# Computing one layer for half the tokens with the tokens in the partitions

## The chip, the cores and the metric

The kernel runs on one core of a Trainium2 chip. The metric is the time of one execution on the device in microseconds (us); the median of three runs is taken. Engines: TensorE (PE; PEld is its weight load), VectorE (DVE), ScalarE (ACT), GpSimd (POOL) and SyncE (SP), which issues the DMAs here.

## What is computed

x has 1024 tokens of 256 features, in float32. Block 1 is a gated layer in which one matrix per expert, ctx_2048[e] (256 x 256), is gate, up and down weight alike; the expert follows from the token's id. Block 2 is a mixture of 16 experts with 96 hidden features, top 4, and a shared expert.

```python
def _L0_xattn_ref(hidden_states, token_ids, Wg, Wu, Wd):      # all three are ctx_2048
    expert_ids = jnp.minimum(tid // tokens_per_expert, E - 1)  # E = 4
    for e in range(E):
        g = jax.nn.silu(jnp.einsum('bsd,fd->bsf', hidden_states, Wg[e]))
        u = jnp.einsum('bsd,fd->bsf', hidden_states, Wu[e])
        y = jnp.einsum('bsf,df->bsd', g * u, Wd[e])
        out = jnp.where((expert_ids == e)[..., None], y, out)
    return out
x = x + _L0_xattn_ref(_layernorm(x, axis=-1), itok_BxS_13_99985, ctx_2048, ctx_2048, ctx_2048)
x = x + _L0_ffn_ref(_layernorm(x, axis=-1), ...)   # sigmoid router, top 4, 16 experts and a shared one
```

Gate and up have the same weights, so layer 1 of block 1 is one product z = W x, from which silu(z) * z is made; layer 2 multiplies that by W again.

## The kernel before

**Tiling.** Tokens are handled in two halves of 512 (h = 0, 1), feature-major: 128 features (m or k = 0, 1) in the partitions, 512 tokens in the columns. Every product has both operands split into a high part rounded for the fast matmul (hi) and the rest (lo): three matmuls hi x hi, lo x hi, hi x lo for each k. The low parts of the weights are made by GpSimd (low_part(n), one for each piece of weights that was loaded), the high parts by ScalarE (high_part(n)).

**Block 1.** The list mixes gives the order of (layer, half, output features m): (1,0,0), (1,0,1), (1,1,0), (2,0,0), (2,0,1), (1,1,1), (2,1,0), (2,1,1). For a mix n TensorE (mix(n)) makes z for each of the 4 experts in a bank of its own, in a ring of 6 PSUM banks (ring_order); ScalarE copies the first expert's (first_z), VectorE puts the others over it where the id is beyond a threshold (pick: copy_predicated, one instruction of 512 columns for each of 3 experts, in a chain). In layer 1 follow silu (silu_z), the product (hidden_product), and the split into h_hi (hidden_high on ScalarE or hidden_cast on VectorE) and h_lo (hidden_low). In layer 2 the residual is added into xt, x with the features in the partitions (add_block_1).

**The norm ahead of block 2, half 0.** It needs tokens in the partitions: TensorE turns x1 (x1_transposes, 8 transposes, inside mix(5)), VectorE takes statistics (tile_stats, layer_norm_vars), GpSimd makes rstd (rstd_of(2)), VectorE and ScalarE normalise two tiles each (layer_norm_apply, apply_norm), and TensorE turns them back (norm_transposes, behind mix(6)'s k = 0 matmuls). Half 1's goes over HBM (turn_x1, write_x1, read_x1, turn_xn, write_xn, read_xn) while block 2 runs. The tile x[:, TT:] serves as the buffer of both turns.

**Block 2.** 26 items (half, chunk of hidden features), in the order (0,0) to (0,10), (1,0), (0,11), (0,12), (1,1) and so on; for item g TensorE does 12 matmuls of gate and up, then the 6 down matmuls of item g - 2. SyncE's queue runs up to 4 items ahead (spread_rows). output(0) adds half 0's result to xt at item 15.

**What sets the order.** Each engine's instructions stand in a list written out by hand; engines wait on semaphores by count. GpSimd's list in the stretch concerned is: low_part(4) to (6), a wait for x1_done (both tiles of half 0's layer 2), low_part(7), rstd_of(2), a wait for xlo_done, further low parts. A piece's load waits until its slot of 4 is free (w_hi, w_lo).

## Time and profile before

| | us |
|---|---|
| median of 3 runs (169.48 to 169.74) | 169.66 |
| the profiled execution | 169.34 |
| its span, first to last instruction | 167.2 |
| TensorE busy, 705 matmuls | 162.5 |
| VectorE busy, 237 instructions | 114.5 |
| ScalarE busy, 116 instructions | 68.7 |
| GpSimd busy, 36 instructions | 37.2 |

The granted TensorE clock was 1.00 throughout. A timeline row has the start, the duration, the engine, the line of the kernel, the operation with output<-inputs, and how many instructions were merged; behind it in brackets stands how long the engine was idle just before, and for whom. Matmuls overlap each other, so their cost is the distance of their starts. All times within the profiled execution are counted from the span's start.

### The profile page before, as it was taken

The numbers are of one execution on the slowest core, as the hardware profiler recorded it, in microseconds if no ns is written. First come the engines' busy times: TensorE is split into PE (matmuls) and PEld (weight loads), VectorE is DVE, ScalarE is ACT, GpSimd is POOL, SyncE is SP. The second block draws the span as 40 slices with busy tenths as digits, with TensorE's granted clock in tenths as the row PEclk, the third lists the DMA queues.
The fourth block names the chain that finished last, engine by engine and source line by source line (L and its number), as shares of the span: only waits on it lengthen the run. The fifth ranks groups of instructions, "written<-read, shape, count | busy, mean of one in ns | idle before, by whom it ended". The sixth has DMA issues, their size and how long they took to land.

```text
span 167.2 us, 2186 instructions
## 1 busy us (share of the span) xinstructions
PE 162.5 (97%) x705; PEld 128.9 (77%) x705; DVE 114.5 (68%) x237; ACT 68.7 (41%) x116; POOL 37.2 (22%) x36
## 2 busy tenths in 40 slices
PE   7999999999999999999999999999999999999992
PEld 2788888888778888888888878888888888888880
DVE  1889999666957998779986744967714444444462
ACT  3654342831359134536734538452222222222210
POOL 1384000656241045556970000000000000000000
PEclk9999999999999999999999999999999999999999
DMA  5891380164304065987225400025441112200003
GB/s 172 275 408 44 107 291 0 21 206 161 115 4 127 16 205 192 219 240 211 67 61 163 153 0 4 1 103 165 173 141 67 63 63 63 65 0 0 4 0 125
DMA packets 12199, 18.78 MB, mean 112 GB/s; under 512 B 3772, under 2 KB 6044, under 8 KB 12060
## 3 DMA queue, kind: packets, MB, share of 16 engines
q1 hardware_dynamic: 12188, 18.64, 34.9%
q8 instruction: 6, 0.10, 0.2%
q14 instruction: 5, 0.04, 0.1%
HBM read 16.39 MB, written 2.24 MB: 111 GB/s over the span
## 4 chain that ended last, share of the span: by engine, by line
PE 95%; DMA 2%; DVE 1%; DVEq 0%; issue 0%
PE bank L1030 23%; PE bank L1131 15%; PE bank L1129 13%; PE bank L1130 13%; PE bank L1149 7%; PE bank L1152 7%; PE bank L1150 7%; DMA first<-first_d 2%; PE bank L998 1%; PE bank L1071 1%; PE bank L1065 1%; PE bank L1126 1%; PE bank L1125 1%; PE bank L987 1%; PE bank L1078 1%; PE bank L1060 1%
## 5 line engine op out<-in xcount | busy, mean ns | idle before, releaser
L1131 PE MATMUL bank<-xn_lo,gu_hi 128*128 128x512 f32 (+1 forms) x104 | 41.1, 395 | 0.0
L1129 PE MATMUL bank<-xn_hi,gu_lo 128*128 128x512 f32 x96 | 38.0, 396 | 0.0
L1130 PE MATMUL bank<-xn_hi,gu_hi 128*128 128x512 f32 x96 | 38.0, 396 | 0.0
L599 ACT ACTIVATE h_hi<-hid 128x512 fp32r<-128x512 f32 (+1 forms) x26 | 16.4, 632 | 45.6 <-DVE hid L860 45.6
L865 DVE TENSOR_TENSOR h_lo<-hid,h_hi 128x512 fp32r<-128x512 f32 (+1 forms) x26 | 18.0, 691 | 14.9 <-ACT h_hi L599 14.9
L1131 PEld LDWEIGHTS bank<-xn_lo,gu_hi 128*128 128x128 f32 (+1 forms) x104 | 19.4, 187 | 4.9
L589 ACT ACTIVATE act_sb<-bank 128x512 f32<-128x512 f32 (+1 forms) x26 | 15.4, 592 | 17.5 <-PE bank L1131 17.4
L472 POOL TENSOR_TENSOR gu_lo<-stage,gu_hi 128x512 fp32r<-128x512 f32 x12 | 17.2, 1457 | 21.7 <-ACT gu_hi L504 16.3
L1129 PEld LDWEIGHTS bank<-xn_hi,gu_lo 128*128 128x128 f32 x96 | 18.0, 188 | 4.4
L1130 PEld LDWEIGHTS bank<-xn_hi,gu_hi 128*128 128x128 f32 x96 | 18.0, 188 | 4.3
L749 DVE COPY_PREDICATED prod<-beyond,bank 128x512 f32<-128x512 uint8 x24 | 17.6, 737 | 5.1 <-PE bank L1030 4.4
L1149 PE MATMUL bank<-h_hi,wd_lo 128*128 128x512 f32 (+1 forms) x52 | 20.6, 396 | 0.0
L1150 PE MATMUL bank<-h_hi,wd_hi 128*128 128x512 f32 (+1 forms) x52 | 20.6, 395 | 0.0
L1152 PE MATMUL bank<-h_lo,wd_hi 128*128 128x512 f32 (+1 forms) x52 | 20.5, 395 | 0.0
L860 DVE TENSOR_TENSOR hid<-prod,bank 128x512 f32<-128x512 f32 x24 | 16.5, 688 | 2.0
L847 DVE TENSOR_TENSOR prod<-act_sb,ids 128x512 f32<-128x512 f32 x12 | 9.6, 796 | 8.6 <-ACT act_sb L589 8.6
L847 DVE TENSOR_TENSOR prod<-act_sb,first 128x512 f32<-128x512 f32 x12 | 10.0, 832 | 6.3 <-ACT act_sb L589 5.7
L1030 PE MATMUL bank<-h_hi,ctx_hi 128*128 128x512 f32 x32 | 12.7, 398 | 0.0
L1030 PE MATMUL bank<-h_lo,ctx_hi 128*128 128x512 f32 x32 | 12.7, 395 | 0.0
L1030 PE MATMUL bank<-h_hi,ctx_lo 128*128 128x512 f32 x32 | 12.7, 395 | 0.0
L1152 PEld LDWEIGHTS bank<-h_lo,wd_hi 128*128 128x128 f32 (+1 forms) x52 | 9.8, 188 | 2.4
L1150 PEld LDWEIGHTS bank<-h_hi,wd_hi 128*128 128x128 f32 (+1 forms) x52 | 9.8, 188 | 2.3
(102 smaller groups left out, 213.2 us busy)
## 6 DMA issues: line engine op xcount, KB each, us to landing
stage<-gu_d SPq DMA_DIRECT2D x6, 512.0 KB, 3.9
stage<-wd_d SPq DMA_DIRECT2D x3, 512.0 KB, 4.3
first<-comb_d SPq DMA_DIRECT2D x8, 192.0 KB, 2.9
ids<-comb_d SPq DMA_DIRECT2D x8, 192.0 KB, 3.3
stage<-ctx_d SPq DMA_DIRECT2D x4, 256.0 KB, 6.0
xt<-xt_d SPq DMA_DIRECT2D x1, 1024.0 KB, 9.9
first<-comb_d SPq DMA_DIRECT2D x8, 128.0 KB, 3.0
ids<-comb_d SPq DMA_DIRECT2D x8, 128.0 KB, 2.9
```

The source lines that it names most:

```text
L472: ins = nc.gpsimd.tensor_tensor(lo[:, s], st[:, s], hi[:, s].bitcast(F32), ALU.subtract)
L749: nc.vector.copy_predicated(prod[:, n % 2], beyond[:, e - 1, h * HALF:(h + 1) * HALF], ring_bank("z", n, e)[:]).then_inc(z_picked, 1)
L847: nc.vector.tensor_tensor(prod[:, g % 2], act_sb[:, g % 2], rows, ALU.mult).then_inc(prod_done, 1)
L860: nc.vector.tensor_tensor(hid[0:w, g % 2], src, up_bank(g)[0:w, :], ALU.mult).then_inc(hid_done, 1)
L865: nc.vector.tensor_tensor(h_lo[0:w, slot[g]], hid[0:w, g % 2], h_hi[0:w, slot[g]].bitcast(F32), ALU.subtract).then_inc(hlo_done, 1)
L1030: return nc.tensor.matmul(ring_bank("z", n, e)[:], (ctx_hi, ctx_lo)[a][:, m, e, k], parts[k][b], start=start, stop=stop)
L1129: nc.tensor.matmul(out[:], gu_lo[:, cols], xn_hi[:, h, k], start=(k == 0), stop=False)
L1130: nc.tensor.matmul(out[:], gu_hi[:, cols], xn_hi[:, h, k], start=False, stop=False)
L1131: ins = nc.tensor.matmul(out[0:rows, :], gu_hi[:, wide], xn_lo[:, h, k], start=False, stop=(k == KC - 1))
L1149: nc.tensor.matmul(acc[k][:], wd_lo[0:w, c, cols], hi, start=(c == 0), stop=False)
L1150: nc.tensor.matmul(acc[k][:], wd_hi[0:w, c, cols], hi, start=False, stop=False)
L1152: ins = nc.tensor.matmul(acc[k][:], wd_hi[0:w, c, cols], lo, start=False, stop=(c == ITEMS - 1))
```

## The change

Layer 2 of half 0 is computed with the tokens in the partitions (row_mix): a tile of the hidden activations of 128 tokens is the stationary operand and ctx of two experts (512 columns) the moving one, so for each of 4 tiles t there are 2 banks ("rows", t, pair) with 6 matmuls each. Mixes (2,0,0) and (2,0,1) leave the list, which has 6 entries now, so the former mix(5) is mix(3), mix(6) is mix(4) and mix(7) is mix(5). The picks of half 0's layer 2 work on rows: 3 instructions of 256 columns for each of 4 tiles, into x1_rows, with a mask of one column broadcast over the features (beyond_rows, from id_rows, which is loaded). x itself comes in rows too (x_rows_d, loaded into the part of xt that half 0 used), and add_rows adds it.

The 8 transposes of x1 are gone; statistics and normalisation read x1_rows in SBUF where they read PSUM. The tokens are in another order in the row tiles: hidden tiles of half 0 are written in four-way runs of 32 columns (hidden()), and the norm transposes write their PSUM columns in runs of 32.

The last sum of half 0 needs x1 feature-major: turn_x0 (8 transposes of 128 x 128 on VectorE at the ends of items 8 and 9), write_x0 (4 DMAs at item 12 of SyncE's list), read_x0 (4 DMAs at item 13), and output(0) waits for them. GpSimd's wait ahead of low_part(7) is for all 4 tiles of rows (row_added). On VectorE, pick(3) of experts 1 and 2 stands ahead of layer_norm_apply(2) and that of expert 3 behind it; on ScalarE silu_z(3) stands behind apply_norm(2).

```diff
+X0_TURN, X0_WRITE, X0_READ = 8, 12, 13
...
+        x1_rows = sb("x1_rows", [P, TT, D])
+        id_rows = sb("id_rows", [P, TT], I32)
+        beyond_rows = sb("beyond_rows", [P, E1 - 1, TT], U8)
...
+        turn_d = nc.dram_tensor("turn_d", (QUARTERS, KC, LANES, HALF), F32, kind="Internal").ap()
...
-                      ("x1", 0, 0, 4), ("x1", 0, 1, 5), ("n2", 0, 0, 4), ("n2", 0, 1, 5)]
+                      ("n2", 0, 0, 4), ("n2", 0, 1, 5)]
...
-        ring_order = [("z", n, e) for n in range(7) for e in range(E1)]
-        ring_order += [("gate", 0, 0), ("up", 0, 0)] + [("z", 7, e) for e in range(E1)]
...
+        ring_order = [("z", n, e) for n in range(3) for e in range(E1)]
+        ring_order += [("rows", t, pair) for t in range(TT) for pair in range(2)]
+        ring_order += [("z", n, e) for n in (3, 4) for e in range(E1)]
+        ring_order += [("gate", 0, 0), ("up", 0, 0)] + [("z", 5, e) for e in range(E1)]
...
+            elif what == "rows" and e == 0:
+                eng.wait_ge(row_first, n + 1)
+                eng.wait_ge(row_picked, n * (E1 - 1) + 1)
+            elif what == "rows":
+                eng.wait_ge(row_picked, (n + 1) * (E1 - 1))
...
+        def hidden(tile, b, at):
+
+            if b >= KC:
+                return tile[:, at]
+            order = "p (b t j) -> p b t j" if tile is hid else "p (t b j) -> p b t j"
+            return tile[:, at].rearrange(order, t=TT, j=LANES)
...
-        mixes = [(1, 0, 0), (1, 0, 1), (1, 1, 0), (2, 0, 0), (2, 0, 1), (1, 1, 1), (2, 1, 0), (2, 1, 1)]
+        mixes = [(1, 0, 0), (1, 0, 1), (1, 1, 0), (1, 1, 1), (2, 1, 0), (2, 1, 1)]
...
-            if n != HALVES:
-                return x[:, n % HALVES * TT + t]
-            at = t % (TT // KC) * D
-            return side_bank("x1", 0, t // (TT // KC))[:, at:at + D]
+            return x1_rows[:, t] if n == HALVES else x[:, n % HALVES * TT + t]
...
-            sp.dma_start(xt[:], xt_d).then_inc(xt_in, 16)
+            sp.dma_start(xt[:, :, HALF:], xt_d[:, :, HALF:]).then_inc(xt_in, 16)
+            sp.dma_start(id_rows[:], id_rows_d).then_inc(id_rows_in, 16)
+            sp.dma_start(xt[:, :, 0:HALF], x_rows_d).then_inc(x_rows_in, 16)
...
+            def write_x0():
+                sp.wait_ge(x0_turned, TT)
+                rows = turn_d.rearrange("q k i (b c) -> b i (q k) c", c=P)
+                blocks = x[:, TT:].rearrange("p t d -> p (t d)").rearrange("p (m c) -> p m c", c=P)
+                for b in range(QUARTERS):
+                    sp.dma_start(rows[b], blocks[b * LANES:(b + 1) * LANES]).then_inc(x0_out, 16)
+
+            def read_x0():
+                sp.wait_ge(x0_out, QUARTERS * 16)
+                rows = turn_d.rearrange("q k i n -> q i k n")
+                for q in range(QUARTERS):
+                    sp.dma_start(xt[q * LANES:(q + 1) * LANES, :, 0:HALF], rows[q]).then_inc(x0_back, 16)
...
+                if g == X0_WRITE:
+                    write_x0()
+                if g == X0_READ:
+                    read_x0()
...
-            pool.wait_ge(x1_done, KC)
+            pool.wait_ge(row_added, TT)
             low_part(E1 + 3)
             rstd_of(2)
...
+            def row_z(t):
+
+                act.wait_ge(row_done, 2 * t + 1)
+                nc.scalar.activation(x1_rows[:, t], ring_bank("rows", t, 0)[:, 0:D], ACT.Copy).then_inc(row_first, 1)
...
+                if n == HALVES:
+                    act.wait_ge(row_added, TT)
...
-                nc.scalar.activation(h_hi[:, b], hid[:, b % 2], ACT.Copy).then_inc(h1_high, 1)
+                nc.scalar.activation(hidden(h_hi, b, b), hidden(hid, b, b % 2), ACT.Copy).then_inc(h1_high, 1)
...
-            first_z(3)
+            row_z(0)
             silu_z(2)
             hidden_high(2)
+            row_z(1)
             high_part(4)
             high_part(5)
+            row_z(2)
             high_part(6)
-            first_z(4)
+            row_z(3)
             high_part(7)
             high_part(8)
             router_low_rows()
-            first_z(5)
-            silu_z(5)
+            first_z(3)
             apply_norm(2)
+            silu_z(3)
             x_high("n2", 0, 0)
             x_high("n2", 0, 1)
-            first_z(6)
+            first_z(4)
             router_logits(0)
             score(0)
             silu_gate(0)
-            first_z(7)
+            first_z(5)
             hid_high(0)
...
-                    dve.wait_ge(side_done, side_at["x1", 0, t // (TT // KC)] + 1)
+                    dve.wait_ge(row_added, t + 1)
...
+            def row_thresholds():
+
+                dve.wait_ge(id_rows_in, 16)
+                for e in range(1, E1):
+                    nc.vector.tensor_scalar(beyond_rows[:, e - 1], id_rows[:], float(e * PER_EXPERT), None,
+                                            ALU.is_ge).then_inc(rows_masked, 1)
+
+            def pick_rows(t, experts=range(1, E1)):
+
+                dve.wait_ge(row_first, t + 1)
+                dve.wait_ge(rows_masked, E1 - 1)
+                for e in experts:
+                    dve.wait_ge(row_done, 2 * t + e // 2 + 1)
+                    if e > 1:
+                        dve.wait_ge(row_picked, t * (E1 - 1) + e - 1)
+                    z = ring_bank("rows", t, e // 2)[:, e % 2 * D:(e % 2 + 1) * D]
+                    nc.vector.copy_predicated(x1_rows[:, t], beyond_rows[:, e - 1, t:t + 1].to_broadcast([P, D]),
+                                              z).then_inc(row_picked, 1)
+
+            def add_rows(t):
+
+                dve.wait_ge(row_picked, (t + 1) * (E1 - 1))
+                dve.wait_ge(x_rows_in, 16)
+                residual = xt[:, t * D // HALF, t * D % HALF:][:, 0:D]
+                nc.vector.tensor_tensor(x1_rows[:, t], x1_rows[:, t], residual, ALU.add).then_inc(row_added, 1)
+
+            def turn_x0(first):
+
+                dve.wait_ge(xn_out, QUARTERS * 16)
+                blocks = x[:, TT:].rearrange("p t d -> p (t d)").rearrange("p (q k t i) -> p t k q i", k=KC, t=TT, i=LANES)
+                for t in range(first, first + 2):
+                    for k in range(KC):
+                        ins = nc.vector.transpose(blocks[:, t, k],
+                                                  x1_rows[:, t, k * P:(k + 1) * P].rearrange("p (q i) -> p q i", i=LANES))
+                    ins.then_inc(x0_turned, 1)
...
-                nc.vector.tensor_scalar(h_hi[:, b], hid[:, b % 2], 1.0, None, ALU.mult).then_inc(h1_high, 1)
+                nc.vector.tensor_scalar(hidden(h_hi, b, b), hidden(hid, b, b % 2), 1.0, None, ALU.mult).then_inc(h1_high, 1)
...
-                nc.vector.tensor_tensor(h_lo[:, b], hid[:, b % 2], h_hi[:, b].bitcast(F32),
+                nc.vector.tensor_tensor(hidden(h_lo, b, b), hidden(hid, b, b % 2), hidden(h_hi, b, b).bitcast(F32),
...
+                if h == 0:
+                    dve.wait_ge(x0_back, QUARTERS * 16)
...
+            row_thresholds()
             pick(2, masked[1])
-            pick(3, masked[0], [1])
+            pick_rows(0, [1])
             hidden_product(2)
-            pick(3, masked[0], [2])
+            pick_rows(0, [2])
             hidden_low(2)
-            pick(3, masked[0], [3])
-            add_block_1(3)
-            pick(4, masked[0])
+            pick_rows(0, [3])
+            add_rows(0)
+            for t in range(1, TT):
+                tile_stats(2, t - 1)
+                pick_rows(t)
+                add_rows(t)
+            tile_stats(2, TT - 1)
+            layer_norm_vars(2)
+            pick(3, masked[1], [1, 2])
+            layer_norm_apply(2)
+            pick(3, masked[1], [3])
+            hidden_product(3)
+            hidden_cast(3)
+            hidden_low(3)
+            x_low("n2", 0, 0)
+            x_low("n2", 0, 1)
+            pick(4, masked[1], [1])
+            turn_logits(0)
+            pick(4, masked[1], [2])
+            normalise_scores(0, mark_best(0))
+            pick(4, masked[1], [3])
             add_block_1(4)
             pick(5, masked[1], [1])
-            for t in range(TT):
-                tile_stats(2, t)
-            layer_norm_vars(2)
+            hidden_2(0)
             pick(5, masked[1], [2, 3])
-            layer_norm_apply(2)
-            hidden_product(5)
-            hidden_cast(5)
-            hidden_low(5)
-            x_low("n2", 0, 0)
-            x_low("n2", 0, 1)
-            pick(6, masked[1], [1])
-            turn_logits(0)
-            pick(6, masked[1], [2])
-            normalise_scores(0, mark_best(0))
-            pick(6, masked[1], [3])
-            add_block_1(6)
-            pick(7, masked[1], [1])
-            hidden_2(0)
-            pick(7, masked[1], [2, 3])
-            add_block_1(7)
+            add_block_1(5)
             hid_low(0)
             for g in range(1, N):
...
+                if X0_TURN <= g < X0_TURN + TT // 2:
+                    turn_x0((g - X0_TURN) * 2)
...
-                        ins = nc.tensor.transpose(banks[k][:, t * P:(t + 1) * P], xn[:, t, k * P:(k + 1) * P],
-                                                  consts_sb[:, 0:P])
+                        out = banks[k][:, t * P:(t + 1) * P]
+                        if n == HALVES:
+                            out = banks[k][:].rearrange("p (b t j) -> p t b j", t=TT, j=LANES)[:, t]
+                        ins = nc.tensor.transpose(out, xn[:, t, k * P:(k + 1) * P], consts_sb[:, 0:P])
...
-            def x1_transposes(h, pair):
...
+            def row_mix():
+
+                hi, lo = ([w[:, b].rearrange("p (t c) -> p t c", c=P) for b in range(KC)] for w in (h_hi, h_lo))
+
+                def moving(w, pair, k):
+                    return w[:, :, 2 * pair:2 * pair + 2, k].rearrange("p m e f -> p e m f")
+
+                for t in range(TT):
+                    for pair in range(2):
+                        wait_ring_read(pe, "rows", t, pair)
+                        out = ring_bank("rows", t, pair)[:].rearrange("p (e m f) -> p e m f", e=2, m=KC)
+                        for k in range(KC):
+                            if t == 0 and pair == 0:
+                                pe.wait_ge(h1_high, k + 1)
+                            nc.tensor.matmul(out, hi[k][:, t], moving(ctx_hi, pair, k), start=(k == 0), stop=False)
+                            nc.tensor.matmul(out, hi[k][:, t], moving(ctx_lo, pair, k), start=False, stop=False)
+                            if t == 0 and pair == 0:
+                                pe.wait_ge(h1_done, k + 1)
+                            ins = nc.tensor.matmul(out, lo[k][:, t], moving(ctx_hi, pair, k), start=False, stop=(k == KC - 1))
+                        ins.then_inc(row_done, 1)
 
...
-            for n in range(2, 5):
-                mix(n)
-            mix(5, {1: lambda: (x1_transposes(0, 0), x1_transposes(0, 1))})
-            mix(6, features=[0])
+            mix(2)
+            row_mix()
+            mix(3)
+            mix(4, features=[0])
             norm_transposes("n2", 2, 0)
-            mix(6, experts=[0, 1], features=[1])
+            mix(4, experts=[0, 1], features=[1])
             gate_or_up(0, False)
             gate_or_up(0, True)
-            mix(6, experts=[2, 3], features=[1])
-            mix(7)
+            mix(4, experts=[2, 3], features=[1])
+            mix(5)
...
+        "id_rows_d": ids[0:HALF].reshape(QUARTERS, TT, LANES).transpose(0, 2, 1).reshape(P, TT),
+        "x_rows_d": a["x"].reshape(TOKENS, D)[0:HALF].reshape(QUARTERS, TT, LANES, D).transpose(0, 2, 1, 3).reshape(P, KC, HALF),
```

## Rows read from the trace of the kernel before

**Rows 1.** The page, part 1: busy us (share of span) and instructions.

```profile
PE 162.5 (97%) x705; PEld 128.9 (77%) x705; DVE 114.5 (68%) x237; ACT 68.7 (41%) x116; POOL 37.2 (22%) x36
```

**Rows 2.** Waits of TensorE: us in total, times, longest.

```profile
PE bank L977 <- DVE warm L874: 1.2, 1, 1.2
```

**Rows 3.** Timeline of TensorE, 24 to 47 us: start us, us, engine, line, operation.

```profile
24.90 0.40 PE L1030 MATMUL bank<-h_hi,ctx_hi 128*128 128x512 f32 x1
...
38.67 0.40 PE L1030 MATMUL bank<-xn_lo,ctx_hi 128*128 128x512 f32 x1
...
40.01 0.39 PE L1030 MATMUL bank<-xn_hi,ctx_lo 128*128 128x512 f32 x1
...
45.37 1.04 PE L987 MATMUL bank<-first,xn 128*128 128x128 f32 x8
...
46.16 0.48 PE L1030 MATMUL bank<-h_hi,ctx_hi 128*128 128x512 f32 x1
...
46.72 0.39 PE L1030 MATMUL bank<-h_lo,ctx_hi 128*128 128x512 f32 x1
```

**Rows 4.** Timeline of VectorE, ScalarE and GpSimd, 25 to 46 us.

```profile
25.56 3.19 DVE L749 COPY_PREDICATED prod<-beyond,bank 128x512 f32<-128x512 uint8 x4
...
28.69 0.69 DVE L757 TENSOR_TENSOR hid<-act_sb,prod 128x512 f32<-128x512 f32 x1
...
29.95 1.51 ACT L504 ACTIVATE gu_hi<-stage 128x448 fp32r<-128x448 f32 x2
...
30.11 0.67 DVE L769 TENSOR_TENSOR h_lo<-hid,h_hi 128x512 fp32r<-128x512 f32 x1
...
30.59 1.22 POOL L468 TENSOR_TENSOR gu_lo<-stage,gu_hi 128x448 fp32r<-128x448 f32 x1 [16.03 <-ACT gu_hi L504]
...
31.73 0.69 DVE L777 TENSOR_TENSOR xt<-prod,xt 128x512 f32<-128x512 f32 x1
...
31.77 3.05 POOL L472 TENSOR_TENSOR gu_lo<-stage,gu_hi 128x512 fp32r<-128x512 f32 x2
...
33.60 0.75 DVE L749 COPY_PREDICATED prod<-beyond,bank 128x512 f32<-128x512 uint8 x1 [1.18 <-PE bank L1030]
...
37.91 2.54 POOL L472 TENSOR_TENSOR wd_lo<-stage,wd_hi 128x512 fp32r<-128x512 f32 x2 [2.38 <-DVE xt L777]
...
41.94 1.01 POOL L478 TENSOR_TENSOR rstd<-vareps,power 128x4 f32<-128x4 f32 x1 [1.49 <-DVE vareps L678]
...
44.37 0.68 DVE L757 TENSOR_TENSOR hid<-act_sb,prod 128x512 f32<-128x512 f32 x1
...
45.55 0.69 DVE L769 TENSOR_TENSOR h_lo<-hid,h_hi 128x512 fp32r<-128x512 f32 x1
```

**Rows 5.** Groups of VectorE by line and form: busy us, mean ns, idle.

```profile
L749 DVE COPY_PREDICATED prod<-beyond,bank 128x512 f32<-128x512 uint8 x24 | 17.6, 737 | 5.1 <-PE bank L1030 4.4
...
L872 DVE TENSOR_TENSOR xt<-bank,xt 128x256 f32<-128x256 f32 x2 | 0.8, 420 | 0.7 <-PE bank L1152 0.7
...
L791 DVE STREAM_TRANSPOSE first<-xn 128x256 f32<-128x256 f32 x4 | 1.4, 404 | 0.0
```

**Rows 6.** Timeline of GpSimd and VectorE, 60 to 79 us.

```profile
60.63 2.99 POOL L472 TENSOR_TENSOR gu_lo<-stage,gu_hi 128x512 fp32r<-128x512 f32 x2 [9.75 <-ACT gu_hi L504]
...
60.86 1.61 DVE L847 TENSOR_TENSOR prod<-act_sb,first 128x512 f32<-128x512 f32 x1 [0.18 <-DMA first<-comb_d]
...
77.10 1.40 DVE L670 BATCH_NORM_STATS2 stats<-first 128x6 f32<-128x256 f32 x4
```

**Rows 7.** Timeline of GpSimd and VectorE, 13 to 16 us.

```profile
13.53 1.03 POOL L478 TENSOR_TENSOR rstd<-vareps,power 128x4 f32<-128x4 f32 x1
...
15.32 2.20 DVE L749 COPY_PREDICATED prod<-beyond,bank 128x512 f32<-128x512 uint8 x3
```

**Rows 8.** Timeline of SyncE's queue, 18 to 21 us.

```profile
19.08 0.81 SPq L368 DMA_DIRECT2D stage<-gu_d  x2
```

**Rows 9.** Stretches: us, busy us (x) of PE, PEld, DVE, ACT, POOL, clock.

```profile
90.00:110.00 20.00, 20.00 (x88) 15.90 (x87) 12.48 (x37) 10.91 (x19) 0.00 (x0) 1.00 0.19 57
```

37 lines of the change are left out of this document (17 added, 20 removed).

## The prediction

> **What bounds the kernel now.** I read the busy line first, then who waited, then the timeline around the step that changes. TensorE is busy 97% of the span [rows 1]. Its longest wait for another engine is 1.2 us, for the warm-up's operand ahead of all work [rows 2]. So no work can be shortened off TensorE's queue to any effect: the time moves only if TensorE gets fewer or slower instructions, or a new wait. Its matmuls of 512 columns follow each other at a fixed step: from the first one of layer 2 at 24.9 us to the one at 38.67 us there are 59 steps, 13.77 / 59 = 0.2334 us [rows 3]. The number in the duration column (0.40) is latency, not cost. Everything else has to be checked for one thing only: does it deliver before TensorE comes for it?
>
> **What TensorE saves.** Layer 2 of half 0 is 2 mixes x 4 experts x 2 k x 3 terms = 48 matmuls of 512 columns before, and 4 tiles x 2 pairs x 2 k x 3 = 48 of 512 columns after. That is no change in count. Removed are the 8 transposes of x1. From the matmul ahead of them (38.67) to the second one behind (40.01) are 1.34 us, where two plain steps would be 0.47 [rows 3]: they cost 0.87 us, and that is all there is to gain. The 8 transposes of the norm (45.37, next matmul 46.16) stay; only the order of their output columns in PSUM differs.
>
> The moving operand of the new matmuls is read in runs of 128 columns, four runs, each 256 apart or more; the trace has no such matmul. The nearest row is the 0.2334 step, and I take it; the bound above is a step twice as long, 11.2 us. Below nothing there is no bound to look for, since the columns are as many. The norm transposes write four runs of 32. The Trainium skill (PSUM — Partial Sum Buffer, Specifications) says that any non-contiguous access pattern in PSUM slows matmuls significantly, which speaks against these; no row of before shows it. The next part will show TensorE waiting right behind these transposes, so even twice their 0.87 us would be hidden.
>
> **What TensorE will wait for.** Behind 48 + 24 matmuls without a break, mix(3) ends 0.87 us earlier than its counterpart did. mix(4) with k = 0, the norm transposes and then mix(4) with k = 1 follow. That last part reads the hidden tile (1,1,1): its low part, done at 45.55 + 0.69 = 46.24 before, was asked for by the matmul at 46.72 [rows 3, 4]. After the change it is asked for at 46.72 - 0.87 = 45.85. The question is when VectorE delivers it, so I walk VectorE's queue.
>
> *Up to the first row.* The chain of four picks starts at 25.56 and takes 3.19 us, so one pick to the next that waits for it is (3.19 - 0.74) / 3 = 0.81, of which 0.74 is the instruction [rows 4, 5]. The three tiny masks (row_thresholds) go ahead of it, 4 columns each: bounds nothing and three times the 0.42 of 256 columns [rows 5]; being 64 times smaller they get 0.3. pick(2) is then done at 28.2. From the end of the third pick (27.9) to the product (28.69) are 0.76; from there to hidden_low 1.42; from there to the add, with one pick between, 1.62 [rows 4], 0.27 less with a pick of half the columns (below). So the product stands at 29.0, hidden_low(2) at 30.4, and the add of row tile 0 at 30.4 + 1.35 = 31.7.
>
> *One row tile.* A tensor_tensor takes 0.69 us for 512 columns (31.73) and 0.42 for 256 [rows 4, 5]: 0.27 per 256 columns. A pick of 256 is then 0.74 - 0.27 = 0.47, and 0.54 to the next in the chain. The mask is broadcast along the row, which no row of before shows: bounds 0.40 (the shortest instruction of 256 columns, [rows 5]) and 0.74, and I take 0.47, since only the width differs from a pick. Per tile: three picks 1.62, the add 0.42, bn_stats about 0.35 (four in 1.40, [rows 6]), three waits of 0.06: 2.45 us, with TensorE delivering one tile in 12 x 0.2334 = 2.8. TensorE is ahead all the time, so the walk is VectorE's own. From 31.7 the last add would end at 31.7 + 0.4 + 3 x 2.45 = 39.5.
>
> *GpSimd in between.* The adds read two SBUF tiles, and so do GpSimd's low parts. At 60.86 such an instruction of VectorE took 1.61 us and not 0.69: GpSimd was inside an instruction begun at 60.63, and VectorE finished about 0.6 behind its end [rows 6, 4]. A pick, which reads one tile from PSUM, took its usual 0.75 at 33.60, while GpSimd was still on the piece begun at 31.77 (two parts, to 34.8) [rows 4]. ScalarE's copy of piece 4 moves from 29.95 to about 30.55 (masks +0.3, row copy +0.3), so GpSimd's low part of 1.22 us goes from 31.2 to 32.4 [rows 4]. The first add, due at 31.7, meets it and ends at 32.4 + 0.3 = 32.7 and not 32.1: +0.6. The halves of piece 5 (2.54 / 2 each, as at 37.91) run to 35.2; the second add, due at 34.8, ends at 35.5: +0.35 more. The other two meet nothing. The last row is added at T = 39.5 + 1.0 = 40.5 us.
> The Trainium skill says this of the port pair in "SBUF — State Buffer", Who interferes with whom: a VectorE instruction with two SBUF inputs and a GpSimd instruction that reads SBUF block each other for a whole instruction. The row at 60.86 agrees.
>
> *From T to the hidden tile.* GpSimd's queue has low_part(7) ahead of rstd_of(2), and low_part(7) now waits for the last row. Before, it started at 37.91, took 2.54 and left GpSimd idle for 1.49 before the rstd at 41.94 [rows 4]. Now it starts at T, so the rstd is out at T + 0.05 + 2.54 + 0.04 + 1.01 = T + 3.64. The variances, ready some 1.3 us behind T, no longer decide. VectorE's queue stands in layer_norm_apply(2) for it, and behind that are queued the last pick of mix(3), the product, the cast and hidden_low(3). From the end of an rstd (13.53 + 1.03) to the pick behind the apply at 15.32 are 0.76; the pick is 0.74; silu, as above, lets the product start 0.76 later; product to hidden_low was 45.55 - 44.37 = 1.18, and that one takes 0.69 [rows 4, 7]. Sum: T + 3.64 + 0.76 + 0.74 + 0.76 + 1.18 + 0.69 = T + 7.77 = 48.3 us. TensorE wanted it at 45.85: a wait of about 2.4 us, in two pieces (the high part first, for two matmuls).
> The time moves by T + 7.77 - 45.85 - 0.87 = T - 38.95, or by -0.87 if T is below 38.1. At T = 40.5: +1.55 us. x_low behind hidden_low(3) is needed only nine matmuls later, and the router's chain starts from TensorE's gate matmuls, so both shift with TensorE. No second wait follows.
>
> **Edits at nothing.** The early loads move the same bytes in one DMA more. If the rstd row, waited for until about 19.08, came 0.3 later, VectorE's scale would slip, but it finishes its hidden tiles at 24.47, ahead of the thresholds, where TensorE asks at 26.07: 1.6 us of cover [rows 4, 8]. Half 0's residual goes over HBM in items 8 to 13: 8 transposes on VectorE, some 2 us by the 0.40 of one of twice their size [rows 5], in a stretch where it is busy 12.5 of 20 us [rows 9] and TensorE uses its hidden tiles two items later. They wait for xn's rows to be out, one item earlier work. SP waits in write_x0 and read_x0 with spread_rows(13) and write_rows(1) queued behind; the product of item 13 needs them some 10 us later. If that cover were gone, the price is a DMA's 2 to 3 us. ScalarE's first_z(3) stands behind two copies of pieces; it is due at 37.7 and I place those at 37.6.
>
> **Rivals.**
> Forecast: T = 40.5, +1.55 us. Chance 0.50.
> Adds not held by GpSimd (ScalarE's copies come at other moments): T = 39.5, +0.55, 170.2 us. For it: both collisions hang on half a microsecond. Chance 0.15.
> Faster: the rows end early, T below 38.6. It needs 1.9 us of the 12 picks, 4 adds and 2 collisions; with picks at the lower bound (0.07 x 12 = 0.8) and no collision (1.0) T is 38.7. At the end, no wait at all, it is -0.87: 168.8 us. Decided by whether the rstd leaves GpSimd before 38.6 + 3.64 = 42.2. Chance 0.17; between this and the next, no measurable change, 0.08.
> Broadcast masks make a pick as dear as one of 512 columns: + 12 x 0.27 = 3.2 more, 174.4 us. Chance 0.07.
> TensorE's step grows with the broken moving operand: up to 2.4 us over 48 matmuls (0.05 each) is hidden in the wait; doubled it is + 11.2 - 0.87 = +10.3. Chance 0.03.
> That the change is not what it says has no room here: the transposes go.
>
> **The numbers.** The profiled run took 169.34 us, with a span of 167.2 and 2.1 around it; the median of the runs is 169.66, 0.3 above. The profiled one would become 170.9, the median 171.2. A measurement of this kernel tells a change from none at about 0.2%, 0.34 us. Slower: 0.50 + 0.15 + 0.07 + 0.03 = 0.75; within 0.08; faster 0.17. The range takes in T from 38.3 to 42.1, so 169.0 to 172.8; it leaves out about half of the faster case and the two dear ones.
>
> **What would show it.** A wait of TensorE of 2 to 2.5 us at the first matmuls of mix(4) with k = 1, named VectorE's h_hi and h_lo; no wait in the row mix; a step of 0.233 there; GpSimd's rstd straight behind low_part(7), with VectorE idle for it; the first two adds of rows at about 0.8 us and the last two at 0.42; picks of rows at 0.47. I am wrong if the rstd ends before 42.2, or if TensorE waits in the row mix or in the items.

## The result, and the profile after

| | before | after |
|---|---|---|
| median of 7 runs of each, taken in turn | 169.48 us | 170.23 us (169.97 to 170.86) |
| ratio, 95% interval | | 1.0047 (1.0028 to 1.0067) |
| the profiled execution / its span | 169.34 / 167.2 | 170.86 / 168.7 |

The change costs 0.75 us. The forecast was slower by 1.55 us. The mechanism is the forecast one, as the rows below and the experiments show; its size is about half. The profiled execution of after is the slowest of its seven, and its numbers lie nearer to the forecast than the median does; why is the first thing that the experiments had to settle.

The page of after, part 1 (as [rows 1]), and TensorE's waits (as [rows 2]):

```profile
PE 162.4 (96%) x697; PEld 127.7 (76%) x697; DVE 118.6 (70%) x256; ACT 69.0 (41%) x118; POOL 37.0 (22%) x36
...
PE bank L1133 <- DVE h_hi L848: 1.6, 1, 1.6
PE bank L1068 <- DVE warm L961: 1.2, 1, 1.2
PE bank L1081 <- DVE xn L770: 0.2, 1, 0.2
```

The 8 transposes are gone (705 - 697 instructions), and one new wait of 1.6 us has come: for h_hi, VectorE's high part of the hidden tile of mix(3). (The 0.2 for xn belongs to the norm of block 1, ahead of 25 us.)

TensorE in after, 25 to 50 us (as [rows 3]); L1110 is the first matmul of the row mix, L1133 those of mix(3) and mix(4), L1228 the first of block 2:

```profile
25.08 0.39 PE L1110 MATMUL bank<-ctx_hi,h_hi 128*128 128x512 f32 x1
...
36.27 0.40 PE L1133 MATMUL bank<-xn_hi,ctx_hi 128*128 128x512 f32 x1
...
44.68 1.12 PE L1081 MATMUL bank<-first,xn 128*128 128x128 f32 x8
...
47.38 0.50 PE L1133 MATMUL bank<-h_hi,ctx_hi 128*128 128x512 f32 x1 [1.59 <-DVE h_hi L848]
...
48.11 0.50 PE L1133 MATMUL bank<-h_lo,ctx_hi 128*128 128x512 f32 x1
...
49.14 0.39 PE L1228 MATMUL bank<-xn_hi,gu_hi 128*128 128x512 f32 x1
```

The row mix is 48 steps in 36.27 - 25.08 = 11.19 us, 0.233 each: the step did not grow. Before, the same stretch (first matmul of half 0's layer 2 to the first one of block 2) ran from 24.90 to 47.64:

```profile
47.64 0.40 PE L1125 MATMUL bank<-xn_hi,gu_hi 128*128 128x512 f32 x1
```

That is 22.74 us before and 49.14 - 25.08 = 24.06 in this execution of after, +1.32. This stretch is the measure used below, because it leaves out what happens before it, which differs between executions.

VectorE and GpSimd in after (as [rows 4]):

```profile
24.99 1.09 DVE L784 TENSOR_SCALAR beyond<-ids 128x512 uint8<-128x512 int32 x3
...
31.81 1.12 DVE L825 TENSOR_TENSOR x_rows<-x_rows,xt 128x256 f32<-128x256 f32 x1
...
34.89 0.73 DVE L825 TENSOR_TENSOR x_rows<-x_rows,xt 128x256 f32<-128x256 f32 x1
...
39.95 0.42 DVE L825 TENSOR_TENSOR x_rows<-x_rows,xt 128x256 f32<-128x256 f32 x1
...
44.01 0.16 DVE L762 SCALAR_TENSOR_TENSOR shift<-meanvar,rstd 128x4 f32<-128x4 f32 x1 [0.75 <-POOL rstd L515]
...
47.36 0.69 DVE L854 TENSOR_TENSOR h_lo<-hid,h_hi 128x512 fp32r<-128x512 f32 x1
...
31.50 1.16 POOL L505 TENSOR_TENSOR gu_lo<-stage,gu_hi 128x448 fp32r<-128x448 f32 x1 [16.48 <-ACT gu_hi L541]
32.60 2.74 POOL L509 TENSOR_TENSOR gu_lo<-stage,gu_hi 128x512 fp32r<-128x512 f32 x2
...
40.45 2.56 POOL L509 TENSOR_TENSOR wd_lo<-stage,wd_hi 128x512 fp32r<-128x512 f32 x2 [4.22 <-DVE x_rows L825]
42.96 1.02 POOL L515 TENSOR_TENSOR rstd<-vareps,power 128x4 f32<-128x4 f32 x1
```

The reader sees three things. The first two adds take 1.12 and 0.73, the last (and the third, not shown) 0.42: the first two meet GpSimd's low parts. The last row is added at T = 40.37, GpSimd had been idle for 4.22 us waiting for it, and puts low_part(7) of 2.56 us ahead of the rstd. VectorE waits for that rstd, so the low part of the hidden tile ends at 48.05 = T + 7.68.

No wait of TensorE in the list above names the round trip of x over HBM, whose DMAs SyncE issues from 97.07 and from 100.93 us on. Behind the stretch the two kernels take the same: from the first matmul of block 2 to the end of the span are 167.2 - 47.64 = 119.6 us before and 168.7 - 49.14 = 119.6 after.

### The profile page after: what moved, and what is told of

The parts are those of the page before. It is cut to its first block, busy times and chain, and to the rows that moved or that the text cites. A ratio compares the mean times of both kernels' runs of the same rounds, so it can differ in the third digit from the quotient of the medians.

```text
span 168.7 us, 2207 instructions
## 1 busy us (share of the span) xinstructions
PE 162.4 (96%) x697; PEld 127.7 (76%) x697; DVE 118.6 (70%) x256; ACT 69.0 (41%) x118; POOL 37.0 (22%) x36
## 4 chain that ended last, share of the span: by engine, by line
PE 70%; DVE 8%; issue 2%; POOL 1%; ACT 1%; DVEq 0%
PE bank L1234 14%; PE bank L1232 13%; PE bank L1233 13%; PE bank L1252 7%; PE bank L1255 7%; PE bank L1253 7%; PE bank L1133 5%; DVE x_rows L817 3%; DVE prod L798 2%; DVE x_rows L825 2%; PE bank L1229 1%; PE bank L1228 1%; DVE hid L842 1%; POOL wd_lo L509 1%; ACT act_sb L608 1%
## 5 line engine op out<-in xcount | busy, mean ns | idle before, releaser
L633 ACT ACTIVATE act_sb<-bank 128x512 f32<-128x512 f32 (+1 forms) x26 | 15.4, 592 | 17.0 <-PE bank L1234 16.9
L798 DVE COPY_PREDICATED prod<-beyond,bank 128x512 f32<-128x512 uint8 x18 | 13.1, 732 | 1.2 <-PE bank L1133 0.7
L1252 PEld LDWEIGHTS bank<-h_hi,wd_lo 128*128 128x128 f32 (+1 forms) x52 | 9.8, 188 | 2.4
L1133 PE MATMUL bank<-xn_hi,ctx_hi 128*128 128x512 f32 x24 | 9.6, 399 | 0.0
L1133 PE MATMUL bank<-xn_hi,ctx_lo 128*128 128x512 f32 x24 | 9.5, 396 | 0.0
```

Source lines behind the costliest of these rows:

```text
L798: nc.vector.copy_predicated(prod[:, n % 2], beyond[:, e - 1, h * HALF:(h + 1) * HALF], ring_bank("z", n, e)[:]).then_inc(z_picked, 1)
L1133: return nc.tensor.matmul(ring_bank("z", n, e)[:], (ctx_hi, ctx_lo)[a][:, m, e, k], parts[k][b], start=start, stop=stop)
L1252: nc.tensor.matmul(acc[k][:], wd_lo[0:w, c, cols], hi, start=(c == 0), stop=False)
```

## The experiments

Theory A, the prediction's: the time is set by the chain of picks, adds (two of them held by GpSimd), low_part(7), rstd and hidden tile; it moves one for one with T. Rivals: the broken operand and output patterns cost something, the round trip over HBM costs something, or the loss lies elsewhere and the wait at h_hi only sits beside it. "Stretch" is the distance defined above, of the profiled execution, as a difference to the 22.74 of before; "T'" is T less the start of the row mix.

**again: the changed kernel, unedited.**

> The changed kernel once more, unedited, for a second trace and the size of its spread. My theory (the time follows T, the end of the last row's add): TensorE's wait for h_hi, 1.59 us and then more for h_lo in the first trace, where T was 40.4, differs from trace to trace with T, h_hi being ready 7.0 us behind T each time; the first trace was of a slow execution (170.86 against a median of 170.23), so this one should show T near 39.8 and a wait about 0.6 us shorter. Rival (T is the same in every execution, and the executions differ somewhere else, at the start or the end): T is 40.4 again whatever the time. Median expected at +0.5 to +0.9 us on before by both.

170.23 us against 169.36, ratio 1.0045 (1.0031 to 1.0060). The profiled execution took 169.91. Its rows:

```profile
24.06 1.09 DVE L784 TENSOR_SCALAR beyond<-ids 128x512 uint8<-128x512 int32 x3
25.07 0.31 DVE L805 TENSOR_SCALAR beyond_rows<-id_rows 128x4 uint8<-128x4 int32 x3
25.28 2.41 DVE L798 COPY_PREDICATED prod<-beyond,bank 128x512 f32<-128x512 uint8 x3
...
30.88 1.13 DVE L825 TENSOR_TENSOR x_rows<-x_rows,xt 128x256 f32<-128x256 f32 x1
...
39.03 0.43 DVE L825 TENSOR_TENSOR x_rows<-x_rows,xt 128x256 f32<-128x256 f32 x1
...
46.46 0.50 PE L1133 MATMUL bank<-h_hi,ctx_hi 128*128 128x512 f32 x1 [1.08 <-DVE h_hi L848]
```

T is 39.46 here, and the wait 1.08. From VectorE's first threshold mask to T are 39.46 - 24.06 = 15.40 us; in the first execution 40.37 - 24.99 = 15.38. So the walk itself is constant, and what differs is when VectorE comes to it: 0.69 us ahead of TensorE's row mix (which started at 24.75) in this one, 0.09 ahead in the other, 0.52 ahead before. That comes from the first microseconds. There the weights of block 1 arrive a little earlier or later from one execution to the next, and GpSimd's low parts of ctx start with them. GpSimd's second rstd stands in its list behind these low parts, and the first instruction of VectorE that uses it is shift. The first execution of after, and then again:

```profile
9.23 3.81 POOL L505 TENSOR_TENSOR ctx_lo<-stage,ctx_hi 128x512 fp32r<-128x512 f32 x3 [1.50 <-ACT ctx_hi L541]
...
15.05 0.16 DVE L762 SCALAR_TENSOR_TENSOR shift<-meanvar,rstd 128x4 f32<-128x4 f32 x1
...
7.99 3.81 POOL L505 TENSOR_TENSOR ctx_lo<-stage,ctx_hi 128x512 fp32r<-128x512 f32 x3 [0.30 <-ACT ctx_hi L541]
...
14.28 0.14 DVE L762 SCALAR_TENSOR_TENSOR shift<-meanvar,rstd 128x4 f32<-128x4 f32 x1
```

The first mask comes 24.99 - 15.05 = 9.94 and 24.06 - 14.28 = 9.78 us behind it; in all traces of this document that distance lies between 9.78 and 10.05. No run moved these low parts on purpose, so this cause is read from the traces and not tested.

Stretch: +0.74. The median of the kernel differs from before's by 0.75 and 0.87, but this execution is 0.3 us faster than its own median, so the near equality is in part chance. What the trace shows without it: the stretch is the only place behind 25 us where after and again differ from before, the rest of the span being 167.8 - 48.23 = 119.6 again.

**psum_add: the second operand of the four adds from PSUM.**

```diff
-                eng.wait_ge(row_picked, (n + 1) * (E1 - 1))
+                eng.wait_ge(row_added, n + 1)
...
-                residual = xt[:, t * D // HALF, t * D % HALF:][:, 0:D]
+                residual = ring_bank("rows", t, 1)[:, 0:D]
```

> add_rows reads its second operand from a PSUM bank of the same tile's picks in place of x's rows in SBUF (the residual is left out of the computation, a wrong addend stands in its place); the bank is kept until the add has read it. So each add has one SBUF input. My theory (the first two adds were held by GpSimd's low parts, 1.12 and 0.73 us for 0.42): all four adds take 0.42, T is 1.0 us earlier, and the time falls by 1.0 us, or by 0.5 or so if typical executions met less of the collision than the traced one. Rival (the long adds have another cause, such as the landing of x's rows): the adds stay long, the time within 0.2 us of the changed kernel.

169.35 us against 169.36, ratio 1.000 (0.9985 to 1.0016). All four adds take 0.42, with GpSimd inside its low part as before:

```profile
31.61 0.42 DVE L825 TENSOR_TENSOR x_rows<-x_rows,bank 128x256 f32<-128x256 f32 x1
...
38.73 0.42 DVE L825 TENSOR_TENSOR x_rows<-x_rows,bank 128x256 f32<-128x256 f32 x1
...
31.30 1.16 POOL L505 TENSOR_TENSOR gu_lo<-stage,gu_hi 128x448 fp32r<-128x448 f32 x1 [16.48 <-ACT gu_hi L541]
32.42 2.56 POOL L509 TENSOR_TENSOR gu_lo<-stage,gu_hi 128x512 fp32r<-128x512 f32 x2
...
46.15 0.50 PE L1133 MATMUL bank<-h_hi,ctx_hi 128*128 128x512 f32 x1 [0.50 <-DVE h_hi L848]
```

From the first mask to T are 39.15 - 24.80 = 14.35, 1.05 less than in again, and the time falls by 0.88. So the collisions cost the chain 1.0 us, and the time follows it about one for one. The Trainium skill ("SBUF — State Buffer", Who interferes with whom) says that a VectorE instruction with two SBUF inputs contends with a GpSimd instruction that reads SBUF, and that one with at most one SBUF input does not, outside the modes in which VectorE uses both of its ports. For these adds the pair of kernels agrees: 1.13 us with two, 0.42 with one. That one SBUF input is not always safe is shown in the last section.

**rstd_first: GpSimd's rstd ahead of low_part(7).**

```diff
-            pool.wait_ge(row_added, TT)
-            low_part(E1 + 3)
             rstd_of(2)
             pool.wait_ge(xlo_done, (HALVES + 1) * KC)
-            for n in range(E1 + 4, early_pieces + 4):
+            for n in range(E1 + 3, early_pieces + 4):
```

> GpSimd's rstd_of(2) ahead of low_part(7), which moves behind its next wait; nothing else. My theory (GpSimd's 2.56 us of low_part(7) hold the rstd): the rstd ends near 42.8 and not 44.0, VectorE goes on when its pick of expert 2 ends (43.3), so 0.7 us are gained: 0.7 to 0.8 below the changed kernel, near before. Rival (VectorE's own queue of rows and picks sets the end, GpSimd is beside it): within 0.2 us of the changed kernel.

169.69 us against 169.36, ratio 1.0024 (1.0010 to 1.0037): 0.54 us are won, where 0.7 to 0.8 were expected. In the stretch itself all is won that was lost, -0.02. The wait for h_hi is down to 0.3. But the two low parts now run from 47.57 to 52.64, beside the router of half 0, and a new wait of TensorE stands at 56.22:

```profile
47.57 2.55 POOL L509 TENSOR_TENSOR wd_lo<-stage,wd_hi 128x512 fp32r<-128x512 f32 x2 [5.62 <-DVE xn_lo L775]
50.08 2.56 POOL L509 TENSOR_TENSOR gu_lo<-stage,gu_hi 128x512 fp32r<-128x512 f32 x2
...
50.47 0.99 DVE L883 TENSOR_TENSOR logit<-turned 128x64 f32<-128x64 f32 x1
...
56.22 0.50 PE L1131 MATMUL bank<-h_hi,ctx_hi 128*128 128x512 f32 x1 [0.31 <-DVE prod L796]
```

**psum_add_rstd_first: both edits.**

> Both edits together (the same wrong addend). My theory: T at 39.4, rstd out at 41.8, VectorE's apply starts behind the pick of expert 2 at 42.3 and not 44.0, so TensorE's wait shrinks from 2.2 us in all to about 0.5 and the time is 1.4 to 1.7 below the changed kernel, 0.4 to 0.8 below before. Rival (something beside this wait costs time in the changed kernel, the HBM round trip or the loads): it stays above before.

169.42 us against 169.36, ratio 1.0008 (0.9996 to 1.0019), no better than psum_add alone, and 0.8 below the changed kernel where 1.4 to 1.7 were expected. By the number it is the rival's case (it stays above before), but neither of the causes that the rival named shows in the trace. Here the stretch is -0.88, the whole gain of the transposes, and TensorE never waits for h_hi. It is given back ten microseconds later:

```profile
51.29 1.35 DVE L890 TENSOR_TENSOR biased<-scores,bias 128x64 f32<-128x64 f32 x1
...
50.00 2.56 POOL L509 TENSOR_TENSOR gu_lo<-stage,gu_hi 128x512 fp32r<-128x512 f32 x2
...
56.16 0.50 PE L1131 MATMUL bank<-h_hi,ctx_hi 128*128 128x512 f32 x1 [0.81 <-DVE prod L796]
```

An instruction of 64 columns, 0.21 us in before, took 1.35: it is held until GpSimd's current part ends (50.00 + 2.56 = 52.56). The picks behind it come later by that, and TensorE waits 0.81 us for a bank.

**late_low: as rstd_first, with low_part(8) moved behind the router.**

```diff
-            pool.wait_ge(row_added, TT)
-            low_part(E1 + 3)
             rstd_of(2)
             pool.wait_ge(xlo_done, (HALVES + 1) * KC)
+            low_part(E1 + 3)
+            pool.wait_ge(rows_turned, 1)
             for n in range(E1 + 4, early_pieces + 4):
```

(This is against the changed kernel. The load of piece 12, which needs that piece's slot, moves in SyncE's list to item 2.)

> rstd_first and one edit more: GpSimd's low_part(8) waits until the router's rows are turned (and the load that needs its slot goes behind write_rows(0)). Nothing left out, the row adds still collide as in the changed kernel. In rstd_first 0.3 us of a new wait of TensorE stood near 56 us, behind router instructions of 0.99 and 0.70 us for 0.23 and 0.21 under low_part(8). My theory: that wait is gone, 0.2 to 0.4 below rstd_first, 169.3 to 169.5. Rival (low parts beside the router are harmless, the wait had another cause): the same as rstd_first, 169.7.

169.05 us against 169.35, ratio 0.9980 (0.9965 to 0.9995). That is 0.64 below rstd_first, more than the 0.2 to 0.4 expected. The wait at 56 us is gone, and the stretch is -0.28, 0.26 below that of rstd_first, whose VectorE was 0.26 us ahead of the row mix where it is 0.54 here. So the new wait of rstd_first did come from that one low part; that the one of psum_add_rstd_first did too is read from its row above.

**gaps: GpSimd's low parts placed between the adds; nothing left out.**

```diff
-            for n in range(E1, E1 + 3):
-                low_part(n)
+            pool.wait_ge(row_added, 1)
+            low_part(E1)
+            low_part(E1 + 1, 2)
             pool.wait_ge(row_added, TT)
-            low_part(E1 + 3)
+            low_part(E1 + 2)
             rstd_of(2)
             pool.wait_ge(xlo_done, (HALVES + 1) * KC)
+            low_part(E1 + 3)
+            pool.wait_ge(rows_turned, 1)
...
```

(low_part(n, 2) waits for the 2nd row tile ahead of its first half and for the 3rd ahead of its second. The load of piece 12 moves as in late_low; first_z(3) goes ahead of high_part(8) on ScalarE.)

> Nothing left out. GpSimd's low parts moved off the places where they meet VectorE's two-input work: piece 4 waits for the first row add, the two halves of piece 5 for the second and third, piece 6 for the fourth, then rstd_of(2); piece 7 runs behind x_low, piece 8 behind the router's rows, its successor's load behind write_rows(0). ScalarE copies first_z(3) ahead of piece 8. My theory: all four adds take 0.42, T is 1.0 us earlier than unedited, the rstd leaves GpSimd 1.4 us earlier relative to T, no new wait near 56 us as the two variants with rstd first had (there low parts 7 and 8 ran into the router's small instructions, 1.35 us for 0.21). TensorE's wait for h_hi and h_lo under 0.4 us, time 0.5 to 0.9 below before (168.5 to 168.9). Rival (the 0.87 us of the transposes are not to be had, since what is saved comes back in a later wait that has not shown yet): within 0.2 us of before or above.

168.60 us against 169.31, ratio 0.9964 (0.9945 to 0.9982): faster than both kernels. The stretch is -0.86. Each GpSimd instruction starts right behind an add and ends before the next, all adds take 0.42 or 0.43 (one row shown), and the rstd is out before VectorE asks:

```profile
32.06 0.43 DVE L832 TENSOR_TENSOR x_rows<-x_rows,xt 128x256 f32<-128x256 f32 x1
...
32.57 1.16 POOL L507 TENSOR_TENSOR gu_lo<-stage,gu_hi 128x448 fp32r<-128x448 f32 x1 [17.15 <-DVE x_rows L832]
35.03 1.30 POOL L513 TENSOR_TENSOR gu_lo<-stage,gu_hi 128x512 fp32r<-128x512 f32 x1 [1.30 <-DVE x_rows L832]
...
40.79 1.01 POOL L519 TENSOR_TENSOR rstd<-vareps,power 128x4 f32<-128x4 f32 x1 [0.34 <-DVE vareps L734]
...
45.08 1.04 PE L1088 MATMUL bank<-first,xn 128*128 128x128 f32 x8
45.88 0.48 PE L1140 MATMUL bank<-h_hi,ctx_hi 128*128 128x512 f32 x1
```

The last two rows say more. With no wait behind them, the 8 norm transposes take 0.80 us to the next matmul, and [rows 3] 46.16 - 45.37 = 0.79 before. Writing PSUM in four runs of 32 columns costs TensorE nothing here. In after this could not be seen, since TensorE waited behind them. The sentence of the Trainium skill quoted in the prediction (PSUM — Partial Sum Buffer, Specifications) would make these transposes dearer; the measurement decides against it for this pattern. It speaks of PSUM alone; that the moving operand read from SBUF in four runs costs nothing either is shown by the step of 0.233.

**gaps_order: in addition VectorE picks expert 3 ahead of layer_norm_apply(2), and silu_z(3) stands ahead of apply_norm(2).**

> As the run gaps, and besides the last pick of mix(3) ahead of layer_norm_apply(2) on VectorE and silu_z(3) ahead of apply_norm(2) on ScalarE, so that the normalisation lies in VectorE's wait for the silu. My theory: h_lo is ready another 0.7 us earlier, so the wait on it is gone if any was left; the transposes of the norm may wait up to 0.3 for ScalarE's tiles. 0.7 to 0.9 below before. Rival: the order of these makes the norm late, TensorE waits for xn 0.5 us or more, and the time is above that of gaps.

168.68 us against 169.31, ratio 0.9960 (0.9947 to 0.9974), stretch -0.89, where 0.7 to 0.9 below before were expected and 0.63 came. No difference to gaps: with no wait left in the stretch there is nothing for it to win.

**before_twice: the kernel before with its 8 transposes of x1 made twice.**

```diff
-                for t in range(TT // KC):
+                for t in list(range(TT // KC)) * 2:
```

> The kernel before with each of the 8 transposes of x1 issued twice, so 8 more. My theory (they cost TensorE their place in its queue, 0.6 to 0.87 us): +0.6 to +0.9 us on before. The first and last of such a group carry more than the middle ones, so 16 in one group may cost less than twice 0.87. Rival (they are partly hidden, so that taking them out gives less than priced): +0.3 or less.

170.32 us against 169.31, +1.01, ratio 1.0068 (1.0051 to 1.0085); stretch 49.15 - 25.54 = 23.61, +0.87. The stretch grows by exactly the 0.87 us of the prediction, which is the price of the eight; the median, at 1.01, is just above the 0.6 to 0.9 expected.

```profile
39.31 0.39 PE L1030 MATMUL bank<-xn_lo,ctx_hi 128*128 128x512 f32 x1
39.54 1.91 PE L1010 MATMUL bank<-first,xt 128*128 128x128 f32 x16
...
41.52 0.39 PE L1030 MATMUL bank<-xn_hi,ctx_lo 128*128 128x512 f32 x1
```

**no_x0: without turn_x0, write_x0 and read_x0.**

> The changed kernel without the way of half 0's x1 over HBM: turn_x0, write_x0, read_x0 and the wait on them left out, so output(0) adds x's rows in place of x1. My theory (hidden at nothing): within 0.2 us of the changed kernel, its wait for h_hi the same. Rival (VectorE's 1.8 us and SyncE's blocked queue in items 8 to 13 cost something): 0.3 us or more below.

170.54 us against 169.35, ratio 1.0072 (1.0047 to 1.0098), stretch +0.73. Stretch and rest of the span (167.8 - 48.23 = 119.6) are those of again, so the round trip costs nothing that can be measured. Why the median is 0.3 above that of again, with intervals that overlap, outside of the 0.2 expected and on the side that the rival did not name, is open.

**stats_twice: tile_stats of the first three row tiles made twice.**

```diff
                 tile_stats(2, t - 1)
+                dve.wait_ge(dstep, steps[0])
+                tile_stats(2, t - 1)
```

> The changed kernel with the statistics of row tiles 0, 1 and 2 taken twice, each time one bn_stats of 0.43 us and its wait more on VectorE. My theory (each us on VectorE's row chain comes out of the end one to one): T later by 3 x 0.45 = 1.35 less up to 0.3 of the second collision, so +1.0 to +1.4 us on the changed kernel, 171.2 to 171.6. Rival (the chain of rows has slack, something else ends the wait): under +0.5.

172.76 us against 169.31, +3.45, ratio 1.020 (1.0171 to 1.0229). Expected were +1.0 to +1.4 over again. The mask-to-T walk grew by 41.24 - 24.23 - 15.40 = 1.61 us, the second add now being held longer (0.97 and not 0.74); the time grew by 2.6 over again. Most of the rest is TensorE's clock. It waited 0.82 us for xn ahead of the norm transposes and 1.59 behind them, and then the step was 0.43 us and not 0.233 for eight matmuls:

```profile
45.49 1.15 PE L1083 MATMUL bank<-first,xn 128*128 128x128 f32 x8 [0.82 <-DVE xn L770]
48.23 0.50 PE L1135 MATMUL bank<-h_hi,ctx_hi 128*128 128x512 f32 x1 [1.59 <-DVE h_hi L848]
...
49.30 0.63 PE L1135 MATMUL bank<-h_hi,ctx_hi 128*128 128x512 f32 x1
...
52.71 0.39 PE L1236 MATMUL bank<-xn_lo,gu_hi 128*128 128x512 f32 x1
```

The stretches of that execution (the eighth column is the granted clock):

```profile
48.00:50.00 2.00, 1.77 (x5) 1.19 (x6) 1.97 (x4) 0.46 (x1) 0.00 (x0) 0.82 0.00 0
50.00:52.00 2.00, 2.00 (x6) 1.47 (x6) 0.84 (x2) 0.14 (x1) 1.82 (x2) 0.50 0.03 8
```

From 49.30 to 52.71 are 3.41 us for 8 steps, 1.87 at the usual rate: 1.54 us lost at the lower of the two clock levels, 1.2 GHz. 1.61 + 1.54 is 3.15, and the profiled execution is 173.27 - 169.91 = 3.36 above that of again. The six runs agree: the three with a mean clock of 0.99 took 172.9 to 173.3 us, the other three (0.997 to 1.0) 171.8 to 172.6.

**stats_once_more: only tile 2's statistics twice.**

> The changed kernel with the statistics of row tile 2 alone taken twice: 0.38 to 0.45 us more on VectorE's row chain, behind both collisions. stats_twice made 1.35 us of such work into 2.5 us of time, and its trace had TensorE's matmuls at 0.43 us a step, granted clock 0.50, for about 3 us behind the wait. My theory (time follows the chain one to one, and the surplus was the lower clock behind a longer idle): +0.4 us on the changed kernel, 170.5 to 170.7, clock 1.00 in the trace. Rival (each us on the chain costs nearly two, clock or not): +0.7 or more at a clock of 1.00.

171.20 us against 169.35, ratio 1.0121 (1.0086 to 1.0156). In the profiled execution (170.96, clock 1.0) the walk is 0.46 longer, and the stretch +1.64, which is 0.9 above again: 0.46 of it the longer walk, the rest VectorE's later start (0.23 ahead of the row mix and not 0.69). Of the six runs, two had a mean clock of 0.99 and took 172.3 and 172.5, four had 0.997 or more and took 170.7 to 171.3. By its clock, the fall of stats_twice came in these two as well, but no trace was taken of them. The same kernel without the edit had 0.996 or more in all its runs.

This run missed what was expected (+0.4, 170.5 to 170.7). The four executions with the clock of 0.997 or more have a median of 171.0, 0.8 above that of again, and the rival, which said +0.7 or more at a clock of 1.00, has the number. Theory A holds in the trace, where the formula below gives the stretch to 0.01 us, since VectorE's start was late; that the other three executions started as late is not shown, so about 0.3 us of the median stay open. It speaks against the rival that the three executions of stats_twice with the clock of 0.997 or more have a median of 171.97, 1.74 above again for 1.61 us of longer walk.

**All runs in one table** (us). "Masks to T" is from the first threshold mask's start to T; the forecast of the stretch is T' - 14.15 + 0.17, worked out below.

| kernel | masks to T | T' | stretch, forecast | stretch, measured | median, less before's |
|---|---|---|---|---|---|
| after | 15.38 | 15.29 | +1.31 | +1.32 | +0.75 |
| again | 15.40 | 14.71 | +0.73 | +0.74 | +0.87 |
| no_x0 | 15.38 | 14.71 | +0.73 | +0.73 | +1.19 |
| psum_add | 14.35 | 14.13 | +0.15 | +0.16 | -0.01 |
| stats_once_more | 15.86 | 15.63 | +1.65 | +1.64 | +1.85 |
| stats_twice | 17.01 | 16.32 | +2.34 | +2.92 | +3.45 |
| rstd_first | 15.37 | 15.11 | | -0.02 | +0.33 |
| late_low | 15.40 | 14.86 | | -0.28 | -0.30 |
| psum_add_rstd_first | 14.35 | 14.06 | | -0.88 | +0.06 |
| gaps | 14.37 | 14.14 | | -0.86 | -0.71 |
| gaps_order | 14.40 | 14.32 | | -0.89 | -0.63 |
| before_twice | | | | +0.87 | +1.01 |

The formula holds for the kernels in which the rstd stands behind low_part(7), to 0.02 us, except stats_twice, where the clock adds 0.58 (49.30 to 50.58 for three steps of 0.233). In the last column rstd_first and psum_add_rstd_first stand above their stretch by the waits at 56 us, 0.31 and 0.81. From the first matmul of block 2 to the end are 119.5 to 119.6 us in all traces but three: 120.1 and 120.6 in these two, and 120.5 in stats_twice, where the clock was still low at the start of it.

## Why the prediction was right in kind and wrong in size

**Right, with the number forecast beside it.** The transposes cost 0.87 (0.87, before_twice). The step of the row mix stayed at 0.233, with no wait in it. The first two adds were held for 0.70 and 0.31 us, 1.01 in all (1.0); without that the time falls by 0.88. A pick of rows took 0.43 to 0.45, no more than the 0.47 that its width gave, so broadcasting the mask costs nothing. From T to the end of the hidden tile's low part are 7.67 (7.77). The rstd came straight behind low_part(7) with VectorE idle for it. The edits put at nothing cost nothing (no_x0 for the round trip, and the equal rest of the span for all behind the stretch). No second wait followed. TensorE's loss in the stretch, 0.87 more than the difference, was 2.19 us in the first execution and 1.61 in again (2.4). The faster rival wanted an rstd before 42.2; it ended at 43.06 in again.

**Wrong: T.** The step that failed is the walk "up to the first row" and its continuation over the row tiles: 40.5 - 24.38 = 16.1 us from the first mask to T, where all five executions with the same row walk (after, again, no_x0, rstd_first, late_low) show 15.4. The forecast of +1.55 hung on this T one for one. Its terms:

| term | forecast | measured (again) |
|---|---|---|
| the three tiny masks | 0.3 | 0.04 (first mask to pick(2) 1.22, 1.18 before) |
| hidden_low(2) to the first add | 1.35 | 1.09 |
| three row tiles, without collisions | 3 x 2.45 = 7.35 | 7.45 - 0.31 = 7.14 |
| collisions | 1.0 | 1.01 |

The masks were priced by their duration. All three together do have one of 0.31, but they start at 25.07, ahead of the end of the large masks (25.15), and pick(2) starts at 25.28, 0.13 behind that end, where it was 0.09 before: the durations of neighbours overlap, and what counts is the distance of starts. The 1.35 came from a distance in before, from hidden_low over a pick to the add, that had gaps in it: the pick started 0.75 behind hidden_low (30.86 and 30.11), where it does so 0.60 behind it in again (30.39 and 29.79); for whom it waited in before the rows don't say. The row tile was counted as three steps of 0.54, where the add follows the third pick at once: 1.54 for the three and 0.04 to the add, and the next pick starts 0.34 behind the statistics. Both terms were upper bounds, used as if they were the value. Together 0.26 + 0.26 + 0.21 = 0.73 us, the main part of the error. (Two slips in the working: the three waits of 0.06 enter the sum as 0.06 in all, and piece 5's low parts, placed to 35.2, would end at 32.4 + 2.54 = 34.9 by their own terms; put right, they move T by +0.36 and by about -0.3 and nearly cancel.)

**The account closes.** The forecast in the stretch's terms: T' + 7.67 - (45.85 - 24.90) - 0.87 = T' - 14.15. To it comes what the forecast left out, 0.17 us: the matmul that waits for h_lo starts 0.06 behind the end of h_lo (47.19 against 47.13 in again), and its follower comes 0.34 behind it (47.53) and not 0.233. The +1.55 becomes: - 0.73 (walk), - 0.10 (T to the tile), - 0.17 (VectorE 0.69 and not 0.52 ahead of TensorE), + 0.17 = +0.72, against 0.74 in again's stretch. With the start of the first execution (0.09) the same sum is 1.55 - 0.73 - 0.10 + 0.43 + 0.17 = +1.32, as measured. For a median execution the start isn't known; with the forecast's own 0.52 the sum is +0.89, inside the intervals of both comparisons (0.5 to 1.1 us). So the walk's 0.73 is shown as an error in every trace with this row walk; that the median came out at 0.75 and not at 0.89 is within the noise.

**Also missing: the spread.** The forecast used one distance, 0.52, between VectorE and TensorE, as one execution showed it. It lies between 0.08 and 0.69 in the executions above. While TensorE had the slack, nobody saw it; behind a wait that VectorE sets, it goes into the time. So the first profiled execution, +1.52 on the profiled one of before, looked like the forecast come true and was an outlier: VectorE's start added 0.43 to it against the forecast's, and a row mix that began at 25.08 and not 24.90 another 0.18. And the forecast took a longer wait at its own length, where in stats_twice the clock added 1.54 us to it.

**The rivals.** "Adds not held" was the wrong description for a result of its size (it forecast +0.55, nearer to the median than the forecast itself): both adds were held, and other terms were smaller. The version that TensorE's patterns or the HBM trip cost something is excluded by the step, by gaps' transposes and by no_x0. Picks as dear as 512 columns did not come (0.43 to 0.45).
